# Graph attention in two layers, projection stage: sums of squares by three additions of halves, and value weights with the head index innermost

## What is computed

```python
h = relu(layernorm(x))
x = x + A_norm @ h @ W_in + At_norm @ h @ W_out       # layer 0, rows divided by their sums
h = relu(layernorm(x))
q = (h @ Wq.T).reshape(d, n, h8); k, v the same       # d = 128 "heads", n = 3327, h8 = 8
a = softmax(einsum('dnh,dmh->dnm', q, k) * d**-0.5 + adj + adj, axis=2)
out = einsum('dnm,dmh->dnh', a, v)
x = x + out.reshape(n, h8 * d) @ Wo.T                 # layer 1
```

## Time and profile before

| what | us |
|---|---|
| median of 3 runs | 11439.6 |
| lowest and highest run | 11436.19, 11452.0 |
| the profiled execution, its own time | 11446.91 |
| its span in the profile | 11445.2 |
| PE, DVE, ACT, POOL busy over the span | 10747.6, 10355.4, 10428.5, 6440.7 |
| the projection stage (first product at 520.3, last value copy ends near 729) | 208.7 |

### The profile page before, as it was taken

How to read it: one execution, slowest core, us unless ns; L and a number is a source line. 1 busy time by engine, 2 the same in 40 slices (tenths; PEclk the granted TensorE clock), 3 DMA queues, 4 the chain that set the end, 5 groups by cost and what they waited for, 6 DMA issues and landing times. The chain is left out here.

```text
span 11445.2 us, 545249 instructions
## 1 busy us (share of the span) xinstructions
PE 10747.6 (94%) x216535; PEld 6833.4 (60%) x216535; DVE 10355.4 (90%) x10893; ACT 10428.5 (91%) x9224; POOL 6440.7 (56%) x3236
## 2 busy tenths in 40 slices
PE   8759999999999999999999999999999999999998
PEld 6526666666665666666666666666666666666666
DVE  7679999999998999999998999999999999999997
ACT  3359999999999999999999999999999999999996
POOL 4345555555555555555555555555555555555554
PEclk9889999999999999999999999999999999999999
DMA  6571111111112111111112111111112111111112
GB/s 223 176 249 40 40 40 40 40 40 40 39 41 76 40 40 40 40 40 40 40 40 77 40 40 40 39 40 39 40 40 79 40 40 40 40 40 40 39 40 80
DMA packets 572920, 651.18 MB, mean 57 GB/s; under 512 B 172173, under 2 KB 511251, under 8 KB 566867
## 3 DMA queue, kind: packets, MB, share of 16 engines
q1 hardware_dynamic: 570130, 617.66, 19.4%
q0 software_dynamic: 832, 1.71, 0.0%
HBM read 485.17 MB, written 133.77 MB: 54 GB/s over the span
## 5 line engine op out<-in xcount | busy, mean ns | idle before, releaser
L1074 DVE SCALAR_TENSOR_TENSOR at_double<-attention_adj_t,at_score 128x832 f32<-128x832 f32 x10240 | 9685.7, 1016 | 832.5 <-PE at_score L1019 827.0
L999 POOL TENSOR_TENSOR at_single<-at_single,attention_adj_t 128x832 f32<-128x832 f32 x3072 | 6104.4, 1987 | 4422.1 <-ACT at_single L1088 4390.9
L1091 ACT ACTIVATE at_double<-at_double 128x1664 f32<-128x1664 f32 x5120 | 8097.9, 1632 | 63.7 <-DVE at_double L1074 55.4
L1019 PE MATMUL at_score<-at_q,at_k 128*32 128x512 bf16 (+1 forms) x106496 | 7397.2, 349 | 233.8 <-ACT at_double L1091 171.2
L1035 PE MATMUL at_acc<-at_double,at_v 128*9 128x208 f32 x81920 | 5546.9, 339 | 221.6 <-issue 220.8
L1019 PEld LDWEIGHTS at_score<-at_q,at_k 128*32 128x32 bf16 x106496 | 3668.4, 145 | 2662.5 <-DVE at_double L1074 1152.0
L1088 ACT ACTIVATE at_single<-at_score 128x832 f32<-128x832 f32 x3072 | 2757.6, 898 | 394.2 <-PE at_score L1019 394.2
L1035 PEld LDWEIGHTS at_acc<-at_double,at_v 128*9 128x9 f32 x81920 | 2165.7, 91 | 1244.2 <-issue 278.4
L1035 PE MATMUL at_acc<-at_single,at_v 128*9 128x208 f32 x24576 | 1650.9, 339 | 0.0
L1035 PEld LDWEIGHTS at_acc<-at_single,at_v 128*9 128x9 f32 x24576 | 655.7, 91 | 282.0 <-issue 0.7
L287 POOL TENSOR_TENSOR layer_col_acc<-layer_col_acc,st_a_rows 128x3328 f32<-128x3328 f32 x26 | 189.2, 7278 | 181.0 <-DMA st_a_rows<-in_adj_dram 181.0
(11 more groups left out here) (123 smaller groups left out, 1251.8 us busy)
## 6 DMA issues: line engine op xcount, KB each, us to landing
at_k<-k_parts_scratch SPq DMA_DIRECT2D x1536, 156.0 KB
at_q<-q_parts_scratch SPq DMA_DIRECT2D x4608, 13.0 KB
at_v<-v_scratch SPq DMA_DIRECT2D x512, 112.5 KB
adj_t_scratch<-st_a_t SPq DMA_DIRECT2D x26, 1664.0 KB, 7.6
st_a_rows<-in_adj_dram SPq DMA_DIRECT2D x25, 1663.5 KB, 8.7
attention_adj_t<-adj_t_scratch SPq DMA_DIRECT2D x16, 2080.0 KB, 16.6
attended_scratch<-at_o SPq DMA_DIRECT2D x1920, 7.3 KB
q_parts_scratch<-pr_partsq SPq DMA_DIRECT2D x39, 512.0 KB, 4.6
```

Of the source, the lines that this page charges most:

```text
L999: pool.tensor_tensor(slot(n), slot(n), at[:, plan.chunk[n], :], ALU.mult).then_inc(multiplied, 1)
L1019: last = pe.matmul(score[plan.buffer(n)][32 * t:32 * (t + 1), a:b], keys[:, 32 * t:32 * (t + 1)], q[k][:, a:b], start=True, stop=True, til ...
L1074: dve.scalar_tensor_tensor(out=slot(n), in0=at[:, plan.chunk[n], :], scalar=2.0, in1=score[plan.buffer(n)][:, 0:NB], op0=ALU.mult, op1=ALU ...
L1091: act.activation(doubles[buffer][:], doubles[buffer][:], ACT.Exp).then_inc(exped, 1)
```

## The change

The sum of squares is no longer one reduction. The 1024 squares are added in halves: 512 + 512 into `halves`, 256 + 256 into `quarters`, 128 + 128 into `norm2`, each by a `tensor_tensor` with both inputs in SBUF, each with a semaphore of its own (`halved`, `quartered`, `summed`). VectorE's order in a chunk becomes rest q, halve q, rest k, quarter q, halve k, total q, quarter k, value copy, total k. ScalarE's square waits for `halved` in place of `summed`. The columns of the value weights are written to `w_t` in the order t * 8 + h (ScalarE, once, as a second instruction), so that the value product has the heads innermost and the value copy reads PSUM in order and writes runs of eight.

```diff
@@ finish_first_layer, scalar
-            act.activation(keep["w_t"][:], y[:, 0:6 * BANK], ACT.Copy)
+            act.activation(keep["w_t"][:, 0:4 * BANK], y[:, 0:4 * BANK], ACT.Copy)
+            act.activation(keep["w_t"][:, 4 * BANK:6 * BANK].rearrange("p (t h) -> p h t", h=H),
+                           y[:, 4 * BANK:6 * BANK].rearrange("p (h t) -> p h t", h=H), ACT.Copy)
@@ project
+        halves = [s.sb(f"halves{kind}", [P, W // 2]) for kind in "qk"]
+        quarters = [s.sb(f"quarters{kind}", [P, W // 4]) for kind in "qk"]
...
@@ scalar
-                    act.wait_ge(summed[kind], c + 1)
+                    act.wait_ge(halved[kind], c + 1)
                     act.activation(squares[kind][:], py[kind][:], ACT.Square).then_inc(squared[kind], 1)
@@ vector
-                for kind in range(2):
+
+                def rest_of(kind):
                     dve.wait_ge(squared[kind], c + 2)
                     dve.wait_ge(part3[kind], c + 1)
                     dve.scalar_tensor_tensor(out=by_head(rest[kind]), in0=by_head(py[kind]), scalar=(SCALE, 1.0)[kind],
                                              in1=parts[b][kind][:, 0, :, half, :], op0=ALU.mult,
                                              op1=ALU.subtract).then_inc(rest_left[kind], 1)
-                    dve.tensor_reduce(norm2[kind][:, bass.ds(c, 1), :].rearrange("p o t -> p (o t)"),
-                                      squares[kind][:].rearrange("p (h t) -> p t h", h=H),
-                                      AX_X, ALU.add).then_inc(summed[kind], 1)
+
+                def halve(kind):
+                    dve.wait_ge(quartered[kind], c + 1)
+                    dve.tensor_tensor(halves[kind][:], squares[kind][:, 0:W // 2], squares[kind][:, W // 2:W],
+                                      ALU.add).then_inc(halved[kind], 1)
+
+                def quarter(kind):
+                    dve.wait_ge(halved[kind], c + 2)
+                    dve.wait_ge(summed[kind], c + 1)
+                    dve.tensor_tensor(quarters[kind][:], halves[kind][:, 0:W // 4], halves[kind][:, W // 4:W // 2],
+                                      ALU.add).then_inc(quartered[kind], 1)
+
+                def total(kind):
+                    dve.wait_ge(quartered[kind], c + 2)
+                    dve.tensor_tensor(norm2[kind][:, bass.ds(c, 1), :].rearrange("p o t -> p (o t)"), quarters[kind][:, 0:P],
+                                      quarters[kind][:, P:2 * P], ALU.add).then_inc(summed[kind], 1)
+
+                rest_of(0)
+                halve(0)
+                rest_of(1)
+                quarter(0)
+                halve(1)
+                total(0)
+                quarter(1)
                 dve.wait_ge(product[2], c + 3)
                 dve.wait_ge(value_stored[k % 2], 32 * i + (16 * b + 16))
-                dve.tensor_copy(value[k % 2][:, :, 0:H].rearrange("p t h -> p h t"), by_head(py[2])).then_inc(value_kept, 1)
+                dve.tensor_copy(value[k % 2][:, :, 0:H], py[2][:].rearrange("p (t h) -> p t h", h=H)).then_inc(value_kept, 1)
+                total(1)
```

More of the change, by code:

```diff
@@ L487, in project @@
         rest_left, part2, part3 = [[s.sem(f"{n}_{kind}") for kind in "qk"] for n in ("rest_left", "part2", "part3")]
-        squared, summed = [[s.sem(f"{n}_{kind}") for kind in "qk"] for n in ("squared", "summed")]
+        squared, halved, quartered, summed = [[s.sem(f"{n}_{kind}") for kind in "qk"] for n in ("squared", "halved", "quartered", "summed")]
         value_kept, ones_set, rooted, norm_stored = s.sem("value_kept"), s.sem("ones_set"), s.sem("rooted"), s.sem("norm_stored")
@@ L626, in _ @@
                 dve.sem_inc(rest_left[kind], 1)
+                dve.sem_inc(halved[kind], 1)
+                dve.sem_inc(quartered[kind], 1)
                 dve.sem_inc(summed[kind], 1)
```

## The result

The changed kernel takes 11485.1 us, the median of 6 runs (11481.32 to 11498.73), against 11441.3 for the kernel before in 6 runs: ratio 1.0039, 95% interval 1.0026 to 1.0052. The forecast was 11419 in a range of 11411 to 11465. The kernel became 44 us slower where 21 us less were expected.

The account below looks back on a forecast made before the run. VectorE bound the projection, with a DMA floor 11% behind; pairs falling from 15.57 to 13.90 us save 20.0 us, the first store 1 us: 21 us off the 11439.6 median gives 11419, range 11411 to 11465.

Parts of the forecast that it names:

- (1): Projection, VectorE: each sum as three additions takes 1.16 us in place of 1.84, saving 1.36 us a chunk.
- rival B: Projection: VectorE's two-SBUF-input additions and GpSimd's third parts exclude each other; slower, 11450 or 11490 us; chance 0.36.
- B's sign: Projection: additions or third parts one to two us longer than neighbours of the same form, DMA engines idle longer.
- B's first walk: One projection chunk with turns taken: next rest q at 8.2 us, 0.4 us a chunk more, 11 us in all.
- The second walk: Same chunk, GpSimd also winning the second turn: ends near 9.7 us, 51 us more in all, 11490.
- (2): Projection, VectorE: value copy in runs of 8 takes 1.14 us in place of 1.83, saving 0.69 us a chunk.
- (3): Projection: new waits between additions are covered by operations in between; a hundredth or two may be left over.
- (4): ScalarE's weight copy split in two, at worst twice 1.02 us, covered by 6.15 us of idleness: cost nothing.
- (5): Projection, what is late next: engines could run a pair in 12.0 us, but 512-byte-packet stores need 13.9 us.
- rival C: Projection: stores drain faster when fed without a pause, up to 46 us gained, 11394; chance 0.06.
- A: Projection: the stores bound at 6.95 us a chunk, 21 us less, 11419 us, own range 11411 to 11425; chance 0.50.
- The engines' loop: Projection: rest k, second part k, copy q, square k and waking VectorE take 6.0 us a chunk.

Follow-up runs that it names:

- e3: The changed kernel with GpSimd's third parts replaced by a 4-element subtraction and two memsets of 1024 elements, third parts zero: 11427.9 us, ratio 0.9990.
- e4: Kernel before plus value layout; ScalarE squares heads 4 to 7 into PSUM, VectorE adds halves with one SBUF input, then reduces: 11425.5 us, ratio 0.9986.
- e8: The kernel of e4 with the same bytes of the parts stored in runs of 4096 bytes in place of 512: 11414.6 us, ratio 0.9972.

## Why the prediction was wrong

The step that failed is (1), the price of the additions. It took their durations from two rows of the trace in which GpSimd had no reading operation beside them, and put 2.32 us a chunk for six. These rows were right for what they showed: 0.69, 0.42 and 0.29 us were estimated, and 0.68, 0.41 and 0.28 measured where no turn was lost. In the changed kernel the six take, start to start, 0.60 + 1.84 + 2.54 + 0.42 + 0.34 + 0.19 = 5.93 us. The difference is all there is: the forecast's 5.73 + 3.61 = 9.34 us, the chunk as measured (599.95 to 609.29). What the sum lacked is the wait for GpSimd's reading operations, which it left to rival B and put at nothing in its own.

The mechanism stood among the rivals, as B, and had 0.36. The rule of the Trainium skill that it cited ("SBUF — State Buffer", Who interferes with whom) was borne out in each of its parts: an addition with two SBUF inputs waits for a third part (halve k 2608 ns), one with a single SBUF input does not (679), and GpSimd's writes alone don't hold it up (685). The trace before could not show it, since no VectorE instruction with two SBUF inputs runs beside a reading GpSimd operation in it. The only rows weighed against B were of the one-input kind, and they say nothing about two. What the prediction named as B's sign, additions one to two us longer than their neighbours and DMA engines idle for longer, is what came. B's first walk was also too mild: it let VectorE make four additions in a row after one wait (8.2 us), while GpSimd took the next turn as soon as one addition was through. The second walk, with GpSimd winning the second turn, gave 9.7 us and 51 us in all, and the measured 9.34 and 44 lie near it. The range ended at a chunk of 8.8 us, between the two walks, for no better reason than the share of chance left out.

The other points, by the prediction's steps:

- (2) The value copy: 1.14 us start to start taken, 1.14 measured (607.96 to 609.10), a gain of 0.7 us a chunk. Right, and by itself worth 15 us.
- (3) The waits between the additions: covered, as said. In e3 no wait for them is shown.
- (4) The weight copy: 2.01 us for the 1024 elements with step 8, "at worst twice 1.02", hidden by ScalarE's 5.18 us of idleness before the square root. Right.

```profile
494.13 2.01 ACT L432 ACTIVATE early_w_t<-fl_y 128x1024 f32<-128x1024 f32 x1
495.91 1.08 ACT L434 ACTIVATE all_wo_t<-fl_y 128x1024 f32<-128x1024 f32 x1
...
503.47 0.23 ACT L436 ACTIVATE fl_stats<-fl_stats 128x26 f32<-128x26 f32 x1 [5.18 <-DVE fl_stats L83]
```

- (5) The stores' floor: 13.90 us a pair forecast; 14.07 and 14.15 in e4 and e3, the two in which value stores end VectorE's idle time (DMA share 1.03 in both). Right within 0.25 us, and rival C with its 12 us is out. In e4 the next stage starts 18.2 us earlier (729.77, was 747.92) where A had 21: 12 times 0.17 us are two of the difference, and the drain behind the last store, 23.4 us in place of 22.4, is one more. The median shows 15 us; the remaining 3 lie within its interval of 10 us to either side and were not followed.
- The engines' loop, 6.0 us, was never reached: VectorE's 6.52 us bounds e8.

In the changed kernel the DMA engines drop to a share of 0.77, TensorE waits, and its granted clock is 0.86 of full speed in the window below, a mean of stretches at 2.4 and at 1.2 GHz, where it was 1.00 in the windows before:

```profile
560.00:747.00 187.00, 132.25 (x241) 52.66 (x240) 187.00 (x181) 117.63 (x121) 104.48 (x61) 0.86 0.77 232
```

No cost of this is to be seen: VectorE has no idle time in the 187.00 us, and what lengthens its additions are the third parts, so no slower product held it up.

## What to carry to other kernels

Before work moves from a one-input to a two-input form on VectorE, look at what GpSimd reads at that moment, and not only at the duration of the form where it runs alone: here 2.3 us of additions became 5.9. Where both must be, keep one input in PSUM, or place the additions in the gap between GpSimd's operations, or cut GpSimd's into shorter pieces, if it has the time; all three turned a loss of 44 us into a gain or a tie. None of them beat the value layout alone (0.9987), because the stores stood right behind. And when VectorE shows no idle time, compare instructions of the same shape with each other: a wait for GpSimd is shown as a longer instruction, not as idleness.

## What the runs showed of the hardware

- Turns are taken by whole instructions, and a waiting GpSimd instruction is next after one VectorE instruction, and the other way round: a 256-element addition of 0.41 us lasted 1.92 us beside a third part of 2.13, and 0.47 (quarter q) and 0.89 us (quarter k, 0.41 alone) beside one in four pieces.
- Step matters to writers and readers alike. A VectorE reduction of 1024 elements read with a step of 128 takes 1.91 to 1.92 us, one of 3328 read in order 3.62. A VectorE copy of 1024 elements with an output step of 9 takes 1981 ns, with runs of eight and one left out 1211; a ScalarE copy of 1024 with an output step of 8 takes 2.01 us, its neighbour without a step 1.08.
- Stores of 512-byte runs filled the DMA engines at 286 GB/s; runs of 4096 bytes, with the values' of 4608, moved near 400 when busy, by the estimate above.
